# Rotation stage of a graph-network kernel: its rows ordered by half of a chunk, five levels as two diagonal 64x64 blocks, the last on one block

## The reference

```
def step(mat, t):
    i, j, theta = t
    ri, rj = mat[i], mat[j]
    mat = mat.at[i].set(cos(theta) * ri - sin(theta) * rj)
    mat = mat.at[j].set(sin(theta) * ri + cos(theta) * rj)
    return (mat, None)
mat, _ = jax.lax.scan(step, eye(256), (src, dst, edge_weight))
x = layernorm(x + x @ mat.T)
```

## Time and profile before

| | us |
|---|---|
| median of three runs | 5916.76 (5911.26 to 5916.9) |
| the profiled execution's own time | 5903.53 |
| its span, first to last instruction | 5901.7 |
| PE, DVE, ACT, POOL busy | 4003.0, 3007.7, 1975.2, 3630.7 |
| matmul instructions in the span | 17113 |
| mean granted clock of TensorE | 0.794 |

### The profile page before, as it was taken

One profiled execution on the slowest core, in us unless ns is written; L12 is line 12 of the kernel. 1 busy time (PEld: TensorE's weight loads), 2 busy tenths in 40 slices (PEclk: granted clock), 3 DMA queues, 4 the chain that ended last, 5 costly groups with the idle time before them and its releaser, 6 DMA issues. The chain is left out here.

```text
span 5901.7 us, 73554 instructions
## 1 busy us (share of the span) xinstructions
PE 4003.0 (68%) x17113; PEld 2943.7 (50%) x17121; DVE 3007.7 (51%) x6900; ACT 1975.2 (33%) x4675; POOL 3630.7 (62%) x2851
## 2 busy tenths in 40 slices
PE   5599932398577778777777534445599999645553
PEld 5488831254455554355555433333376777433332
DVE  6576636621455552255555434445367777533334
ACT  0022210010466661166565112221188888200000
POOL 0144422067787754587773788885677777478884
PEclk9999975599788888888887755556799999855655
DMA  0000001333666643466663333333344444243332
GB/s 8 23 11 11 11 14 39 95 81 67 166 176 170 165 113 99 111 176 170 166 165 90 68 80 85 82 85 82 81 120 120 119 119 119 72 103 83 84 83 72
DMA packets 510802, 558.08 MB, mean 95 GB/s; under 512 B 302100, under 2 KB 394239, under 8 KB 510285
## 3 DMA queue, kind: packets, MB, share of 16 engines
q0 software_dynamic: 349600, 362.07, 25.6%
q1 hardware_dynamic: 157688, 186.99, 11.1%
q10 hardware_dynamic: 3250, 6.40, 0.4%
HBM read 460.15 MB, written 92.22 MB: 94 GB/s over the span
## 5 line engine op out<-in xcount | busy, mean ns | idle before, releaser
L1261 POOL DMA_INDIRECT sum_gx_sb<-scratch_xw,keep_k_row_step_sb x1272 | 1588.1, 1248 | 425.2 <-issue 358.6
L1374 PE MATMUL sum_a_ps<-sum_gx_sb,sum_sel_sb 125*125 125x258 f32 (+1 forms) x4320 | 1189.8, 438 | 454.2 <-ACT sum_gx_sb L1310 178.3
L1374 PEld LDWEIGHTS sum_a_ps<-sum_gx_sb,sum_sel_sb 125*125 125x125 f32 x4320 | 917.4, 238 | 641.5 <-issue 451.5
L1310 ACT ACTIVATE sum_gx_sb<-sum_gx_sb,sum_wt_sb 125x129 f32<-125x129 f32 x3312 | 981.8, 388 | 539.0 <-DVE sum_wt_sb L1503 539.0
L2499 POOL DMA_INDIRECT filter_gx_sb<-scratch_h,keep_k_src_step_sb x424 | 603.3, 1423 | 174.3 <-issue 97.8
L1168 POOL DMA_INDIRECT scratch_grouped<-keep_k_value_sb,keep_k_place_sb x400 | 481.1, 1203 | 250.7 <-issue 133.8
L2970 POOL DMA_INDIRECT source_gx_sb<-scratch_h,source_grouped_sb x424 | 529.5, 1249 | 140.1 <-issue 115.7
L2982 PE MATMUL source_s_ps<-source_gx_sb,source_sel_sb 125*125 125x257 f32 x848 | 376.1, 621 | 306.3 <-DMA source_gx_sb<-scratch_h,source_grouped_sb 304.8
L2982 PEld LDWEIGHTS source_s_ps<-source_gx_sb,source_sel_sb 125*125 125x125 f32 x848 | 249.0, 307 | 433.4 <-issue 170.2
L2556 PE MATMUL filter_ps<-filter_m_sb,filter_h_sb 128*125 128x256 f32 x1696 | 385.4, 380 | 1.7 <-DVE filter_h_sb L2626 1.7
L3009 DVE TENSOR_TENSOR keep_agg_sb<-source_s_ps,keep_agg_sb 125x257 f32 x424 | 181.0, 427 | 389.0 <-PE source_s_ps L2982 384.8
(11 more groups left out here) (515 smaller groups left out, 6865.6 us busy)
## 6 DMA issues: line engine op xcount, KB each, us to landing
scratch_hots<-sum_cuts_sb SPq DMA_DIRECT2D x108, 244.1 KB
filter_sel_sb<-scratch_hots SPq DMA_DIRECT2D x106, 244.1 KB
sum_gx_sb<-scratch_xw,keep_k_row_step_sb POOLq DMA_INDIRECT x1272
scratch_xw<-gate_xsb_sb SPq DMA_DIRECT2D x50, 253.9 KB
scratch_xw<-attend_xsb_sb SPq DMA_DIRECT2D x25, 507.8 KB
filter_ea_sb<-in_ea_t SPq DMA_DIRECT2D x424, 24.4 KB
filter_gx_sb<-scratch_h,keep_k_src_step_sb POOLq DMA_INDIRECT x424
source_gx_sb<-scratch_h,source_grouped_sb POOLq DMA_INDIRECT x424
```

What stands on the lines that cost most here:

```text
L1261: nc.gpsimd.indirect_dma_start(out=gx[:, q, j, :], out_offset=None, in_=table, in_offset=bass.IndirectOffsetOnAxis(ap=keep["row_step"][:, ...
L1310: last = nc.scalar.activation(here, here, ACT.Copy, scale=wt[q][:, h, j:j + 1])
L1374: last = mm(psa[b][0:P, half, 0:BF], sel[:, 0, p, j, :], gx[:, q, at, half * BF:(half + 1) * BF], **flags)
```

## The change

The rows of a chunk are ordered by half: i rows and j rows of steps 0 to 31 on partitions 0 to 63, those of steps 32 to 63 on 64 to 127. Levels 0 to 4 join steps only within a half, so X is then made of two 64x64 blocks on the diagonal. They are kept packed: `xc` holds X and its transpose as 128 partitions by 64 columns a chunk, block 0 on the upper and block 1 on the lower partitions. y, z and start_x become 64x64 matmuls with 64 columns, two for each one before, in turn on block 0 and block 1 (a quarter of the array each, on the diagonal). Level 5 has one product on one quarter: `across`, the block of lt that joins the halves. X is put together in `full` by ACT (`fill`), and w reads that. grow_x is one addition a half. POOL multiplies the masks of levels 1 to 4 in one instruction. A no-op that takes the wait (`held`) stands ahead of each group of quarter matmuls.

```diff
-    t = np.arange(R) % K
-    masks = np.zeros((128, LV + 1, G, 128), np.float32)
+    row, at = np.arange(128), np.arange(KH)
+    step_row, step_col = row // K * (K // 2) + row % (K // 2), row[:, None] // K * (K // 2) + at[None, :] % (K // 2)
+    masks = np.zeros((128, LV, G, KH), np.float32)
+    for lv in range(LV - 1):
+        br, bc = step_row[:, None] // (1 << lv), step_col // (1 << lv)
+        masks[:, lv] = ((br + 1 == bc) & (bc % 2 == 1))[:, None, :]
+    masks[:, LV - 1] = (row[:, None] % KH == at[None, :])[:, None, :]
...
-            low, high = slice(0, 64), slice(64, 128)
-            vec.scalar_tensor_tensor(rows_of[low, :], f[0], -1.0, f[0], ALU.mult, ALU.max)
+            halves = [(slice(32 * b, 32 * b + 32), slice(64 * b, 64 * b + 32), slice(64 * b + 32, 64 * b + 64)) for b in range(2)]
+            for at, low, high in halves:
+                vec.scalar_tensor_tensor(rows_of[low, :], f[0][at], -1.0, f[0][at], ALU.mult, ALU.max)
             vec.tensor_scalar(lone[:], f[1], 0.0, float(D), ALU.is_equal, ALU.mult)
             dve.drain()
-            vec.tensor_scalar(rows_of[low, :], rows_of[low, :], 1.0, -1.0, ALU.max, ALU.add)
-            vec.scalar_tensor_tensor(rows_of[high, :], f[1], -1.0, lone[:], ALU.add, ALU.add)
+            for at, low, high in halves:
+                vec.tensor_scalar(rows_of[low, :], rows_of[low, :], 1.0, -1.0, ALU.max, ALU.add)
...
+            for at, low, high in halves:
+                for side in (low, high):
+                    vec.tensor_scalar(col[side, 0, :], f[0][at], 0.0, -1.0, ALU.max, ALU.add)
...
+    lta, ltb, lt = mem.sb("lta", [128, G, R]), mem.sb("ltb", [128, G, R]), mem.sb("lt", [128, G, KH])
+    across = [mem.sb(f"across{q}", [KH, G, KH]) for q in range(2)]
...
+    lm = [mem.sb(f"lm{q}", [128, LV - 1, G, KH]) for q in range(2)]
...
+    xc = [mem.sb(f"xc{q}", [128, 2, 2, G // 2, KH]) for q in range(2)]
+    full = mem.sb("full", [128, G, R])
+    ysb = mem.sb("ysb", [128, 2, G // 2, KH])
...
-                    vec.tensor_tensor(lt[:], lta[:], ltb[:], ALU.add).then_inc(sems["lt_made"], 1)
+                    vec.tensor_tensor(across[q][:], lta[blocks[0], :, blocks[1]], ltb[blocks[0], :, blocks[1]], ALU.add)
+                    for b in blocks:
+                        last = vec.tensor_tensor(lt[b], lta[b, :, b], ltb[b, :, b], ALU.add)
+                    dve.drain()
+                    dve.nop().then_inc(sems["lt_made"], 1)
...
-                last = vec.tensor_tensor(half(xx[q], h), psz[h][:, 0:W2], half(xx[q], h), ALU.add)
-                if lv < LV - 1:
-                    last = vec.tensor_tensor(half(xt[q], h), psz[h][:, W2:2 * W2], half(xt[q], h), ALU.add)
-                last.then_inc(sems["x_grown"], 1)
+                here = xc[q][:, h].rearrange("p o n r -> p (o n r)")
+                vec.tensor_tensor(here, psz[h][:, 0:2 * W2], here, ALU.add).then_inc(sems["x_grown"], 1)
...
-                        for h in range(2):
-                            grow_x(k, u, 5, h)
...
-                for lv in range(1, LV):
-                    last = tt(lm[q][:, lv], lt[:], masks[:, lv], ALU.mult)
-                last.then_inc(sems["lt_masked"], 1)
+                tt(lm[q][:, 1:LV - 1].rearrange("p l g r -> p l (g r)"),
+                   lt[:].rearrange("p g r -> p (g r)").unsqueeze(1).broadcast_to([128, LV - 2, G * KH]),
+                   masks[:, 1:LV - 1].rearrange("p l g r -> p l (g r)"), ALU.mult).then_inc(sems["lt_masked"], 1)
...
+            def fill(k, q):
+
+                act.wait_ge(sems["x_grown"], k * (2 * (LV - 2)) + 2 * LV - 2)
+                for b in blocks:
+                    nc.scalar.copy(full[b, :, b].rearrange("p (h n) r -> p h n r", h=2), xc[q][b, :, 0]).then_inc(sems["full_made"], 1)
+                for h in range(2):
+                    act.wait_ge(sems["z_made"], k * (2 * (LV - 1)) + 2 * (LV - 1) - 1 + h)
+                    nc.scalar.copy(full[blocks[1], 2 * h:2 * h + 2, blocks[0]],
+                                   psz[h][blocks[1], 0:W2].rearrange("p (n r) -> p n r", r=KH)).then_inc(sems["full_made"], 1)
...
-                    for n, g in enumerate(chunks(h)):
-                        last = nc.tensor.transpose(psy[h][:, n * R:n * R + R], xt[q][:, g, :], ident[:])
+                    pe.nop().then_inc(sems["held"], 1)
+                    for n in range(G // 2):
+                        for b in blocks:
+                            last = mm(psy[h][b, n * KH:n * KH + KH], xc[q][b, h, 1, n, :], ident[b, b], start=True, stop=True)
...
-                    for n, g in enumerate(chunks(h)):
-                        last = mm(psy[h][:, n * R:n * R + R], lm[q][:, lv, g, :], xx[q][:, g, :], start=True, stop=True)
+                    pe.nop().then_inc(sems["held"], 1)
+                    for n in range(G // 2):
+                        if lv == LV - 1:
+                            last = mm(psy[h][blocks[1], n * KH:n * KH + KH], across[q][:, 2 * h + n, :], xc[q][blocks[0], h, 0, n, :],
+                                      start=True, stop=True)
+                        else:
+                            for b in blocks:
+                                last = mm(psy[h][b, n * KH:n * KH + KH], lm[q][b, lv, 2 * h + n, :], xc[q][b, h, 0, n, :],
+                                          start=True, stop=True)
                     last.then_inc(sems["y_made"], 1)
 
             def make_z(k, q, lv):
 
+                if lv == 1:
+                    pe.wait_ge(sems["full_made"], k * 4 + 1)
                 for h in range(2):
                     pe.wait_ge(sems["y_copied"], k * (2 * LV) + 2 * lv + h + 3)
-                    if lv == 1:
-                        pe.wait_ge(sems["x_grown"], k * (2 * (LV - 1)) + 1 + h)
-                    for n, g in enumerate(chunks(h)):
-                        last = mm(psz[h][:, n * R:n * R + R], xt[q][:, g, :], ysb[:, g, :], start=True, stop=True)
+                    pe.nop().then_inc(sems["held"], 1)
+                    for n in range(G // 2):
+                        for b in blocks[1:] if lv == LV - 1 else blocks:
+                            last = mm(psz[h][b, n * KH:n * KH + KH], xc[q][b, h, 1, n, :], ysb[b, h, n, :], start=True, stop=True)
                     if lv < LV - 1:
-                        for n, g in enumerate(chunks(h)):
-                            last = mm(psz[h][:, W2 + n * R:W2 + n * R + R], ysb[:, g, :], xt[q][:, g, :], start=True, stop=True)
+                        for n in range(G // 2):
+                            for b in blocks:
+                                last = mm(psz[h][b, W2 + n * KH:W2 + n * KH + KH], ysb[b, h, n, :], xc[q][b, h, 1, n, :],
+                                          start=True, stop=True)
...
-                        pe.wait_ge(sems["x_grown"], k * (2 * (LV - 1)) + 2 * LV)
+                        pe.wait_ge(sems["full_made"], k * 4 + 5)
...
-                            last = mm(psw[:, g, :], xx[u][:, g, :], wt[u][:, g, :], start=True, stop=True)
+                            last = mm(psw[:, g, :], full[:, g, :], wt[u][:, g, :], start=True, stop=True)
```

More of the change, by code:

```diff
@@ L31 @@
 R = 2 * K
+KH = R // 2
 CP, CA = 112, 7
@@ L302, in _ @@
             f = [acc[:, :, n] for n in range(NF)]
-            low, high = slice(0, 64), slice(64, 128)
-            vec.scalar_tensor_tensor(rows_of[low, :], f[0], -1.0, f[0], ALU.mult, ALU.max)
+            halves = [(slice(32 * b, 32 * b + 32), slice(64 * b, 64 * b + 32), slice(64 * b + 32, 64 * b + 64)) for b in range(2)]
+            for at, low, high in halves:
+                vec.scalar_tensor_tensor(rows_of[low, :], f[0][at], -1.0, f[0][at], ALU.mult, ALU.max)
             vec.tensor_scalar(lone[:], f[1], 0.0, float(D), ALU.is_equal, ALU.mult)
             dve.drain()
-            vec.tensor_scalar(rows_of[low, :], rows_of[low, :], 1.0, -1.0, ALU.max, ALU.add)
-            vec.scalar_tensor_tensor(rows_of[high, :], f[1], -1.0, lone[:], ALU.add, ALU.add)
+            for at, low, high in halves:
+                vec.tensor_scalar(rows_of[low, :], rows_of[low, :], 1.0, -1.0, ALU.max, ALU.add)
+                vec.scalar_tensor_tensor(rows_of[high, :], f[1][at], -1.0, lone[at, :], ALU.add, ALU.add)
             dve.drain()
             dve.nop().then_inc(rho_made, 1)
[L311 to L317, removed]
+            for at, low, high in halves:
+                for side in (low, high):
+                    vec.tensor_scalar(col[side, 0, :], f[0][at], 0.0, -1.0, ALU.max, ALU.add)
+                    vec.tensor_scalar(col[side, 2, :], f[1][at], -1.0, None, ALU.add)
+                vec.tensor_scalar(col[low, 1, :], f[2][at], -1.0, None, ALU.add)
+                vec.tensor_scalar(col[high, 1, :], f[3][at], -1.0, None, ALU.mult)
+                vec.tensor_copy(col[low, 3, :], f[3][at])
+                vec.tensor_scalar(col[high, 3, :], f[2][at], -1.0, None, ALU.add)
             dve.drain()
@@ L371, in layer0_turn @@
 def layer0_turn(nc, mem, dr, col, turns, mt):
```

(19 more changed lines are left out.)

13 lines of the change are left out of this document (2 added, 11 removed).

## The result

The changed kernel takes 5875.84 us (median of four runs, 5870.53 to 5878.54) against 5914.88 for the kernel before: ratio 0.9934, 95% interval 0.9916 to 0.9951. A second set of runs on another occasion gave 5864.97 against 5914.21, ratio 0.992 (0.9908 to 0.9932). So it is 39 to 49 us faster. 5867 had been predicted, but that it came so near is in part luck: two terms of opposite sign were off, and they cancelled. Most of this document is about the second, a loss of 16 to 22 us in a phase whose code the change doesn't touch.

A forecast was written before the change was run, and what follows sets the result against it. The prediction took PE's and DVE's chains, side by side, to set the 24.89 us stage. Loop -60, ahead of the loop +4 and PE's clock +6 sum to -50; from 5916.8 that gives 5867 us, range 5842 to 5928.

The forecast's parts named there:

- The quarters run at once: In y, z and start_x on PE, diagonal quarters work together: z from 1.78 to 0.90 us, y to 0.45; chance 0.60.
- The stage: One stage of the rotation loop falls from 24.89 to 22.15 us, which gives 60 us in 22 stages.
- Ahead of the loop: Before the rotation loop: list phase +10.5 us, smaller mask load -3, memset and additions +1.4, POOL's first round -4.8; sum +4.
- The clock: PE's clock in the rotation loop dips in a quarter of the stages, about 1.2 us each: +6, bounds 0 and +26.
- the sum: Whole kernel against the profiled execution of 5903.5 us: -60 + 4 + 6 = -50 us.
- nothing else of the 5901.7 us span is touched but some work just ahead of the loop: Whole kernel: outside the rotation loop and some work just ahead of it, no phase is touched; no time counted there.
- Serial quarters: Rival, chance 0.25: quarters in y and z run one after the other, level 5.1 us, stage 24.8, total 5921.
- Clock stays low: Rival, chance 0.08: small matmuls leave PE at 1.2 GHz in the rotation loop, stage 31 us, total about 6050.
- Each no-op exposes 0.1 us: Rival, chance 0.07: waiting no-ops ahead of quarter matmuls, 20 of them, take 2 us of a stage; gain 10 us.

The follow-up runs named there:

- e10: Changed kernel with each block 0 product in z of levels 1 to 4 issued twice, block 1 once; a stage of 24.05 us.
- e2: Changed kernel with POOL multiplying the masks of levels 1 to 4 in four instructions of 256 elements, not one of 1024; 5876.43 us, ratio 0.9924.
- e7: Changed kernel with 7 no-ops more on DVE at the head of the rotation phase; 5855.19 us, ratio 0.9899.
- e8: Changed kernel with no-ops putting every engine's later code back to its place of before, modulo 8192 bytes; 5854.02 us, ratio 0.9894.
- e3: Changed kernel with a second no-op behind each of the 22 `held` no-ops of a stage; a stage of 21.85 us.
- f1: Changed kernel with pick at the head of a stage on DVE instead of its end; 5849.49 us, ratio 0.9898.
- c2: The changed kernel run again unchanged, with a profile of its own; 5864.97 us, ratio 0.992.
- e9: The kernel before with 121 no-ops on DVE at the head of its rotation phase; 5938.05 us, ratio 1.0035.
- e1: Changed kernel with y, z and start_x going through block 0 first, then block 1, in each group of four matmuls; 5870.32 us.

## Why the prediction came out as it did

- *The quarters run at once* (0.60): right, now from rows of this kernel and from e10. From z's start to u's were 1.08 us (0.90 + 0.18 predicted), from r's start to z's 1.06 (0.87 + 0.15), the level 4.06 (4.09), w came 2.21 us behind y of level 5 (2.4). The Trainium skill, "TensorEngine Tiling (Array Packing)", Key Properties, says that different tiles load and multiply in parallel; the trace agrees, 16 pairs in two quarters in the 0.68 us of 8 in one.
- *The stage:* 22.15 predicted, 21.84 measured. Terms that were off: pick 0.88 (1.25), since POOL was done after 6.03 us and not 6.4, just ahead of pick (e2); the buffer's landing 3.60 (3.77); level 3 4.68 (4.44), as DVE's three additions took 1.2 us. The old stage was 24.74 in the mean, not the 24.86 of the one read. 2.9 us in 22 stages are 64, not 60.
- *Ahead of the loop* +4: measured +3.7, with +10.3 for the list phase, -3 for the smaller load and, as what is left, -3.5 for the rest (+1.4 and -4.8 predicted).
- *The clock* +6: measured 0. The granted clock was 1.00 from 261 to 742 us, through the gaps in level 1.
- So the rotation phase gave -61, where the sum had -50: of the 11 us 4 are the stage's and 6 the clock's.
- **The step that failed** is the first paragraph's "nothing else of the 5901.7 us span is touched but some work just ahead of the loop". The code that is not touched was moved by 448 bytes, and by that four stalls came up just behind a jump back of DVE's loop: +22 us in the second attention round, +16 in the second pair of profiles. No rival held it. Without it (e7, e8) the change gives 59 to 60 us, 5854 to 5855, still inside the range, but 12 us from the forecast. That the forecast was met within 9 us is luck: the rotation phase won 11 us more than the sum had, and the untouched code gave these back.
- *Serial quarters* (0.25): out by e10. Its level was priced well, 5.1 against the 4.98 of e10, though e10 doubles z alone; a stage of 24.05 would still have been a little faster than before.
- *Clock stays low*: out, 1.00 in the loop. *Each no-op exposes 0.1 us*: out for the stage by e3, though in the tail of a stage a second no-op did cost some 0.15 us, which DVE's longer chain hides.

## What to carry to other kernels

Compare two profiles phase by phase over the same instructions, the untouched phases too: a gain that shrinks where nothing was changed is a finding. Look for idle "issue" between two instructions with no wait between them, and test it with a few no-ops that only move the code; this kernel gained or lost 10 to 24 us of some 5900 by that alone, and a small change is judged fairly only with the later code put back. And after one chain has been cut, read which one sets the stage now: here an instruction moved on DVE (f1) took 1.1 us off a stage, where the whole change took 2.9.

## What the runs showed of the hardware

- The stalls of DVE at that line lasted 2.4 to 3.7 us each (changed kernel, c2, e9), beside a load of 8192 bytes of instructions that took 0.31 to 1.61 us. They depend on where the code lies: 7 instructions decide, and a shift by 121 instructions, 7 short of 8192 bytes, does what the change did. The Trainium skill, "Vector Engine (DVE) Microarchitecture Reference", 1.2 Instruction fetch and dispatch (NX sequencer), gives an instruction 64 bytes; the compiled programs agree, 7 no-ops made DVE's 448 bytes longer.
- Quarters of PE on the diagonal run at once in f32: 0.058 us a pair in each, with the other's pair 0.007 us behind. Within a group of four matmuls they need not stand by turns in the program (e1: 1.13 us from z to u, against 1.08).
- An instruction of pick beside a running one of POOL took 1.48 us, behind it 0.48; in e2 it ended 0.28 us behind POOL's, as in the earlier trace rows.
